# Weighted values as 128x128 products from a block-diagonal operand, and batch 6's second layer moved into the pauses of batch 7

## The reference, cut to what matters

```python
def layer0(x, w_qkv0, w_out0, w_qkv1, w_out1):       # 16 heads of 16, no softmax
    # axis 0: each column of the image is a sequence; axis 1: each row is one
    dots = einsum('bhie,bhje->bhij', q, k) * 256 ** -0.5
    out  = einsum('bhij,bhje->bhie', dots, v) @ w_out
    return out_of_columns + out_of_rows

def layer1(x, Wq, bq, Wk, bk, Wv, bv, Wo, bo, sigma):   # one head of 256
    gw = 1 / (2 * sigma ** 2)
    r_attn = softmax(einsum('bhwd,bhkd->bhwk', q, k) - gw * dist)   # along a row
    r_out  = einsum('bhwk,bhkd->bhwd', r_attn, v)
    c_attn = softmax(einsum('bhwd,bgwd->bwhg', q, k) - gw * dist)   # along a column
    c_out  = einsum('bwhg,bgwd->bhwd', c_attn, v)
    return (r_out + c_out) @ Wo.T + bo

x = x + layer0(gn(x), ...)
x = x + layer1(gn(x), ...)
```

## Time and profile before

| quantity | value |
|---|---|
| median of 3 runs | 221.05 us |
| profiled execution, its own time | 221.89 us |
| span of the profile | 219.7 us |
| PE busy | 211.5 us, 96% |
| PE weight loads busy | 180.7 us, 82% |
| DVE busy | 161.6 us, 74% |
| ACT busy | 119.5 us, 54% |
| POOL busy | 44.5 us, 20% |
| granted TensorE clock | 1.000 of full speed, in all 40 slices |

### The profile page before, as it was taken

How to read it: one execution, slowest core, us unless ns; L and a number is a source line. 1 busy time by engine, 2 the same in 40 slices (tenths; PEclk the granted TensorE clock), 3 DMA queues, 4 the chain that set the end, 5 groups by cost and what they waited for, 6 DMA issues and landing times.

```text
span 219.7 us, 9124 instructions
## 1 busy us (share of the span) xinstructions
PE 211.5 (96%) x3718; PEld 180.7 (82%) x3718; DVE 161.6 (74%) x484; ACT 119.5 (54%) x263; POOL 44.5 (20%) x64
## 2 busy tenths in 40 slices
PE   8799799999989999999999999999999999989995
PEld 4447689889968988898979897998898888988983
DVE  5699769667766777688677876787877666857782
ACT  2375474288616872677356853696269625830350
POOL 7500131012401070106010420115010701103000
PEclk9999999999999999999999999999999999999999
DMA  6962420233232342244224422334221421014004
GB/s 220 375 110 70 98 46 0 96 113 60 64 112 97 56 106 80 96 96 96 82 85 108 96 72 84 118 63 106 96 96 17 119 89 66 3 61 86 3 0 96
DMA packets 45568, 19.41 MB, mean 88 GB/s; under 512 B 35568, under 2 KB 41200, under 8 KB 45552
## 3 DMA queue, kind: packets, MB, share of 16 engines
q1 hardware_dynamic: 43872, 17.02, 28.5%
q10 hardware_dynamic: 1680, 2.16, 2.8%
HBM read 7.36 MB, written 3.95 MB: 51 GB/s over the span
## 4 chain that ended last, share of the span: by engine, by line
PE 80%; DVE 10%; DMA 3%; ACT 3%; issue 2%; SPq 0%; POOL 0%; ACTq 0%; DVEq 0%; POOLq 0%
PE bank L1086 42%; PE bank L1159 7%; PE bank L1181 7%; PE bank L1258 6%; PE bank L1190 3%; PE bank L1237 2%; PE bank L1110 2%; DMA turned_values<-v_row 2%; DMA v_col<-turned_values 1%; PE bank L1114 1%; PE bank L1104 1%; PE bank L1099 1%; PE bank L1516 1%; DVE wqkv_lo L883 1%; DVE moments L673 1%
## 5 line engine op out<-in xcount | busy, mean ns | idle before, releaser
L454 ACT ACTIVATE k_v<-bank 128x512 f32<-128x512 f32 x32 | 19.1, 598 | 37.8 <-PE bank L1086 35.6
L465 ACT ACTIVATE kv<-bank,head_scale 128x256 f32<-128x256 f32 x64 | 25.1, 476 | 8.5 <-PE bank L1159 8.5
L367 POOL TENSOR_TENSOR xt_lo<-xn,xn_hi 128x256 fp32r<-128x256 f32 x14 | 13.2, 966 | 56.3 <-DVE xn_hi L725 56.3
L381 POOL TENSOR_TENSOR rstd<-var_eps,minus_half 128x4 f32<-128x4 f32 x8 | 8.1, 1018 | 69.8 <-DVE var_eps L714 69.8
L733 DVE TENSOR_TENSOR kv<-bank,block_mask 128x512 f32<-128x512 f32 x32 | 20.5, 682 | 0.8 <-PE bank L1159 0.7
L1181 PE MATMUL bank<-kv,q 64*32 64x128 f32 x1024 | 18.5, 274 | 1.0 <-DVE kv L733 0.7
L752 DVE TENSOR_TENSOR o_lo<-bank,o_hi 128x256 fp32r<-128x256 f32 x30 | 13.9, 508 | 7.5 <-ACT o_hi L480 7.3
L1159 PE MATMUL bank<-v_wide,k_v 64*32 64x128 f32 x1024 | 18.4, 273 | 0.0
L1159 PEld LDWEIGHTS bank<-v_wide,k_v 64*32 64x32 f32 x1024 | 14.4, 105 | 3.4 <-issue 2.5
L1181 PEld LDWEIGHTS bank<-kv,q 64*32 64x32 f32 x1024 | 14.2, 105 | 3.3 <-issue 1.4
L1086 PE MATMUL bank<-o_hi,wout_hi 128*128 128x256 f32 x60 | 16.9, 281 | 0.0
(11 more groups left out here) (239 smaller groups left out, 584.5 us busy)
## 6 DMA issues: line engine op xcount, KB each, us to landing
v_wide<-k_v SPq DMA_DIRECT2D x61, 64.0 KB, 1.9
turned_values<-v_row SPq DMA_DIRECT2D x7, 258.0 KB, 2.7
v_col<-turned_values SPq DMA_DIRECT2D x14, 129.0 KB
x_blk<-in_x_dram SPq DMA_DIRECT2D x56, 32.0 KB, 1.8
x_kept<-x_chan SPq DMA_DIRECT2D x7, 256.0 KB, 2.3
x_res<-x_kept SPq DMA_DIRECT2D x7, 256.0 KB, 2.2
out_dram<-y_blk SPq DMA_DIRECT2D x56, 32.0 KB, 1.7
wqkv_in<-in_L_conv_w_qkv_dram ACTq DMA_DIRECT2D x2, 384.0 KB, 5.8
```

Of the source, the lines that this page charges most:

```text
L367: pool.tensor_tensor(turn_to(xt_lo[:, c, :]), turn_from(xn[0][:, c, :]), turn_from(xn_hi[0][:, c, :].bitcast(FP32)), ALU.subtract)
L454: act.activation(k_v[:, axis, :, t, :], src[:, :].rearrange("p (i d) -> p i d", i=2), ACT.Copy).then_inc(kv_taken, 1)
L465: last = act.activation(kv[axis][:, 1, :, :, :, head // 2, own].rearrange("p t c s e -> p (t c s) e"), kv_bank[1][:, :].rearrange("p (a e) ...
```

## The change

`weights_t` becomes a tile of 128 x 4 x 128, set to zero once during setup. `scale_raised` is one instruction with no halves. `turn_weights` is four transposes, each of 32 partitions, into the diagonal blocks of `weights_t`. `block_values` makes 8 products with 128 partitions and 128 columns, all into one bank, rows first, columns added on top, and has no `carry()`. One instruction, `final_sum`, adds the residual. The tiles `half`, `half_i`, `spread_out` go.

In turn 7 PE's order becomes: `queries(1)`, `key_value(0)`, `project_t(6)`, `transpose_output(1)`, `queries(0)`, `project_out(1)`, the transposes of line 1445, `project_values(6, 0)`, the products of line 1453, `project_values(6, 1)`, `block_scores(6)`, the group mean, `keep_busy(5)`, the group variance, `keep_busy(10)`, the folded queries of batch 7, values and scores of both tiles, `block_values(6)`, the residual's products, `keep_busy(4)`, and the tiles as before with one `keep_busy(2)`. ACT, DVE and SP follow; two of the eight stores of batch 6 go to ACT's queue, behind batch 7's result. `shift_logits` is cut in two (`add_row_term` is its first instruction).

```diff
@@ setup (DVE)
-            dve.tensor_scalar(half_i[:, :], iota_row[:, :], 5, 1, ALU.logical_shift_right, ALU.bitwise_and)
-            const(dve.tensor_copy(half[:, 1:2], half_i[:, :]))
-            dve.tensor_scalar(half[:, 0:1], half[:, 1:2], -1.0, 1.0, ALU.mult, ALU.add)
+            dve.memset(weights_t[:, :, :], 0.0)
@@ SP, behind the last batch() of the list
+            store_y(LAST - 2, range(1))
             put_values(LAST - 1)
+            store_y(LAST - 2, range(1, CC))
             turn_values(LAST - 1)
-            store_y(LAST - 2)
-            store_y(LAST - 1)
+            store_y(LAST - 1, range(CC), FEW)
@@ ACT, turn 7
             take_even(LAST, 1)
             mask_kv(LAST, 0)
+            split_o(LAST, 1, [bank[0], None])
+            take_even(LAST, 0)
             take_t(LAST - 1)
-            take_values(LAST - 1, 0)
-            split_o(LAST, 1, [bank[0], None])
-            take_values(LAST - 1, 1)
-            take_even(LAST, 0)
...
-            exponentials(LAST - 1)
+            take_values(LAST - 1, 0, late_vp_banks)
+            take_values(LAST - 1, 1, late_vp_banks)
...
             act.activation(t_last[:, 0, :], last_t_bank[0][:, 0:TOKENS], ACT.Identity, bias=c1[:, 0:1]).then_inc(last_t_taken, 1)
+            exponentials(LAST - 1)
...
+            act.wait_ge(out_ready, LAST)
+            for quad in range(QUADS - FEW, QUADS):
+                act.dma_start(block_of(out_dram, LAST - 1, CC - 1, quad), y_blk[quad * QUAD:(quad + 1) * QUAD, CC - 1, :, :]).then_inc(stored, 16)
@@ DVE, functions
             def scale_raised(b):
...
+                dve.tensor_tensor(weights[:, :, :], raised[:, :, :], inverse[:, :].unsqueeze(2).broadcast_to([P, SLOTS, BLOCK]), ALU.mult
+                                  ).then_inc(weight_step, 1)
             def turn_weights(b):
...
+                for quad in range(QUADS):
+                    own = slice(quad * QUAD, (quad + 1) * QUAD)
+                    last = dve.transpose(weights_t[own, :, own], weights[own, :, :])
+                last.then_inc(weights_ready, 1)
+            def final_sum(b, src=pv_bank):
...
+                dve.tensor_tensor(y_chan[:, :, :].rearrange("p c n -> p (c n)"), src[:, :],
+                                  x1b[:, :, :].rearrange("p c n -> p (c n)"), ALU.add).then_inc(out_sum, 1)
@@ DVE, turn 7
-            turn_t(LAST - 1)
             split_o(LAST, 1, [bank[0], None])
             take_odd(LAST, 0)
+            turn_t(LAST - 1)
...
-            shift_logits(LAST - 1)
+            take_scores(LAST - 1, late_s_bank)
             spread(LAST)
             variance(LAST)
-            sum_raised(LAST - 1)
-            scale_raised(LAST - 1)
-            turn_weights(LAST - 1)
+            add_row_term(LAST - 1)
             coefficients(LAST)
...
-            sum_rows(LAST - 1, last_pv_banks)
+            shift_logits(LAST - 1)
             dve.wait_ge(last_t_ready, 2)
             dve.tensor_scalar(t_last[:, 1, :], last_t_bank[1][:, TOKENS:2 * TOKENS], c1[:, 1:2], None, ALU.add).then_inc(last_t_taken, 1)
-            sum_columns(LAST - 1, last_pv_banks)
+            sum_raised(LAST - 1)
+            scale_raised(LAST - 1)
...
+                if t == 0:
+                    turn_weights(LAST - 1)
             for t in range(TT):
                 if t == 1:
-                    turn_y(LAST - 1)
+                    final_sum(LAST - 1, late_pv_bank)
...
+            turn_y(LAST - 1)
@@ PE, block_values
             for axis, values in ((1, v_row), (0, v_col)):
                 for m in range(CC):
                     for t in range(TT):
...
+                        last = pe.matmul(part, values[:, t, m * P:(m + 1) * P], weights_t[:, (1 - axis) * TT + t, :],
+                                         start=(axis == 1 and m == 0 and t == 0), stop=(axis == 0 and m == CC - 1 and t == TT - 1))
```

## The result

| quantity | before | after |
|---|---|---|
| median of 5 runs each | 221.07 us (220.75 to 221.3) | 222.82 us (222.63 to 223.03, and one of 228.97) |
| ratio after / before, 95% | | 1.0081, 1.0067 to 1.0095 |
| profiled execution, its own time | 221.89 us | 222.8 us |
| span of the profile | 219.7 us | 220.6 us |

The kernel became slower by 1.75 us. The forecast was 221.1, no change; 222.82 lies just above the range's upper end of 222.7, and slower had been given 0.27.

A forecast was written before the change was run, and what follows sets the result against it. PE's own time was taken to bound turns 2 to 6, with DVE partly on the path in setup, turns 1 and 7. Terms -1.2 + 0.24 + 0.15 + 0.85 = +0.04 gave 221.1 us, no change; range 219.5 to 222.7.

The forecast's parts named there:

- Passes of 128 columns: Loop `block_values`: 16 passes of 0.111 us replace 32, saving 0.20 a turn, -1.2 us over six turns.
- rival 5: Loop `block_values`: the two 64-row halves had worked side by side, full array twice as slow, 6 x 1.8, 232 us; chance 0.01.
- So it is covered, with 0.3 of slack: DVE in the loop: four weight transposes take 1.04 us, end at 159.86, and PE wants them at 160.16.
- the prediction's own signs of being wrong: PE waiting for DVE's weights in the loop, passes at 0.12 or more, `v_col` before 203.6, or weight transposes waiting for DVE.
- rival 4: Each 32-partition transpose costs as a 128x256 one, 1.8 us in all; PE waits from 1.34 on; 224.7 or 222.9; chance 0.08.
- Setup: DVE's setup path: a 0.50 us memset replaces two `half` instructions of 0.26, +0.24 us, ends -0.1 and +0.42.
- Turn 7 up to the folded queries: Turn 7's new order: PE reaches the folded queries at 203.2 instead of 205.98, 2.8 us earlier.
- +0.15 us: End of turn 7: wait for `v_col`, then transposes and `block_values` on the path; weight transposes at 213.35, before 213.20.
- The bound of +1.0: Upper bound on turn 7's +0.15 us: transposes at 4 x 0.45 and values landing late.
- The stores: End of the kernel: two batch 6 stores behind batch 7's result on ACT, +0.85 us, ends 0 and +1.3.
- Rival 2: The two ACT stores end beside batch 7's own landing, or SP would have ended last: 220.2 us; chance 0.20.
- The base: Whole kernel: sum made against the profiled 221.89 us, 0.84 above the median, and the difference applied to the median 221.05.

The follow-up runs named there:

- values_later: Kernel after with `block_values` moved behind `project_q` in the loop and `final_sum` behind `split_xn` on DVE: ratio to before 1.0036, 222.45 us.
- no_filler: Kernel after without `keep_busy(4)` ahead of the transposes of batch 7's weights: ratio to before 1.0058, 222.82 us.
- stores_between: Kernel after with batch 6's two stores on ACT placed between the two transfers of batch 7's result, not behind both: ratio to before 1.0079, 223.22 us.
- the second pair: Kernel before and kernel after, each unchanged and profiled once more: 221.56 us for before (one execution), 223.74 us and ratio 1.0116 for after.
- products_only: Kernel before with the new products, four transposes, memset and single sum, but turn 7's old order and all stores on SP: ratio 1.0002, 221.8 us.
- order_only: Kernel after with the old products, one transpose and old sums, keeping turn 7's new order and two stores on ACT: ratio to before 1.0047, 222.25 us.
- shift_behind: Kernel after with batch 6's `shift_logits` moved behind the bias of batch 7's folded queries on DVE: ratio to before 1.012, 224.38 us.

## Why the prediction was wrong, point by point

**Passes of 128 columns: right.** 0.113 us each (forecast 0.111), and 0.20 to the next product. 16 passes took 1.81 where 32 had taken 1.93, so the halves had not worked side by side (rival 5), and halving the count gave 0.12 a turn. By the Trainium skill (TensorEngine Tiling (Array Packing), "Instruction Overhead") it would have been some 0.4 a turn, the prediction's estimate by that page; the measurement decides against that figure here.

**"So it is covered, with 0.3 of slack": the step that failed in the loop.** It rested on two estimates, both too low. The four transposes were put at 1.04, by starts every 0.24; they took 1.25, with starts every 0.31. And PE was let start right when they end, a term put at nothing without a reason; in all six turns it started 0.24 or 0.25 behind them. Either error alone would have fitted into the 0.3 of slack; both together made PE start 0.16 later than forecast (159.65 and not 159.25 + 0.24). This PE wait for DVE's weights is the first of the prediction's own signs of being wrong. The upper bound of 1.8 in the prediction and rival 4 named the mechanism, but rival 4's threshold of 1.34 left out the 0.24. The loop gave 0.42 instead of 1.2. `values_later` shows it from the other side: with the weights early, a turn is 0.27 shorter than before, even more than the 0.20 forecast.

**Setup: right in kind, a little high.** +0.18 from `hcol` on, forecast +0.24. The memset's row has 0.48, where 0.50 was put; on the path it cost 0.41, the 0.17 of idle time ahead of it included, and the `half` instructions gave back 0.24 of the 0.26. The first pair of profiles differs by 0.34 at the statistics product and the second by -0.01 (24.74 before, 24.73 after), since `hcol` itself moves by some 0.2 from execution to execution.

**Turn 7 up to the folded queries: right.** To compare with the forecast's clock, 0.85 is added to the times after, as far as the kernel was ahead. The values left for DRAM at 198.46 (forecast 198.4), the folded queries started at 202.43 + 0.85 = 203.28 (203.2), DVE came to the wait at 203.6 (203.6).

**Turn 7 from there: "+0.15 us" failed by 0.8.** Several terms of the same sum were too small, each by a little and all to one side. `v_col` was used at 205.46 and not 205.0: 7.0 us from `put_values` and not 6.6 (DVE stood 1.84; 203.6 to 205.0 in the forecast is 1.4). The weights were ready 1.15 behind the second maximum and not 0.94, PE started 0.11 behind them where nothing was put, and so it began `block_values` at 210.56, not at 209.8. The rest is the 0.1 of `block_values` itself. The bound of +1.0 just held in the first pair of profiles and not in the second (1.4). That PE and not DVE is the later at the weights' transposes was right, as `no_filler` shows, and so was the diagnosis that `block_values` had moved from a stretch of waits onto the path.

**The stores: right.** +0.8 in the profiles and 0.8 by the rows of `stores_between`, forecast +0.85. Rival 2 falls.

**The base.** The prediction made its sum against the profile and applied the difference to the median. This is sound only if the 0.84 between them lies outside the terms. But about half of it or more sat in turn 1, in a landing that took 3.98 in that execution and 3.46 and 3.04 in others. It changes no term of the sum. It explains most of why the two profiles differ by only 0.9 where the medians differ by 1.75.

With the terms as measured the sum is -0.42 + 0.18 + 0.95 + 0.8 = 1.5, and 2.0 with turn 7 as in the second pair; the medians' 1.75 lies between. The products alone brought nothing (`products_only`, 1.0002): setup cost 0.18 more, and the transposes ate most of what the shorter passes won. The order with the stores cost 1.0 us (`order_only`, 1.0047). The forecast had the mechanisms, but put +0.04 where these terms give 1.5 to 2.0: of the difference 0.8 lies in the loop and 0.8 to 1.3 in turn 7. No error to one side was hidden by one to the other.

What stays open: whether the executions of `shift_behind` behind its ratio lost their clock in the same long pause as the profiled one, and why one kernel after stood at 1.0081 and at 1.0116 on two chips, beyond the 0.5 us of later values.

## What to carry to other kernels

A step that feeds PE has to be ready ahead of the product, by 0.24 us in this loop and 0.11 in the straight code of turn 7, and each of several transposes of few partitions costs its own time; count both before calling them covered, and if they are not, move the consumer one product back rather than speed up the producer. A transfer with a variable landing should be issued where nothing waits for it: moved late, its mean and its spread both go onto the path. Before a sum is made against one profile, compare it with a second one: a difference of that kernel to itself may be as large as the terms.

## What the runs showed of the hardware

- The write of 258 KB of values to DRAM landed, in SP's view, in 3.04, 3.46 and 3.98 us at the same place in different executions, and in 3.22, 3.46 and 4.01 in turn 7 of the new order.
- A DVE transpose of 32 partitions and 128 columns took 0.30 us, and four in a row 1.25 with no overlap; one of 128 partitions and 256 columns took 0.45. Four quarters cost 2.8 times the whole.
- From the end of DVE's transposes to the start of the product that waits for them it was 0.24 to 0.25 us in the six loop turns of the kernel after and 0.11 in its turn 7, which is written out. Why the two differ was not tested.
- The zeroing of 128x512 fp32 took 0.48 on DVE and 0.52 on POOL.
- The granted clock fell to 0.50 after PE had stood for 2.46 us (`shift_behind`, one profile). Kernels of the new order ran at a mean granted clock between 0.989 and 0.998 in a part of the executions behind their ratios (`order_only` four of six, at 0.995 and 0.996; `no_filler` five of nine; the kernel after itself one of seven, at 0.998), and the kernel before at 0.998 or more. PE pauses of 1.18 and 1.05 us in turn 7 are new in the kernel after, but in `order_only` the second is 0.23; that the pauses are the cause wasn't tested by itself.
